# A gated network whose down weights are unpacked one step later, with first rows and first queries prepared sooner

## The reference

```python
x = x + L0_xattn(layernorm(x), ctx, ctx, gamma)         # 8 heads across the sequence axis, softmax
x = x + L0_ffn(layernorm(x), gate_up_packed, gate_up_scales, down_packed, down_scales)
x = x + L1_xattn(layernorm(x), ctx, Wq, bq, Wkv, bkv, Wp, bp)    # 16 heads, q, k, v rounded to 8 bits
x = x + L1_ffn(layernorm(x), w1, b1, w2, b2)                      # ternary weights

def L0_ffn(x, ...):                                     # inner width 1408
    w_gu, w_down = dequant_fp4(gate_up_packed), dequant_fp4(down_packed)   # 8 four-bit values a word,
    gate, up = split(x @ w_gu.T)                                           # a scale for each 128 inputs
    h = silu(gate) * up
    y = h @ w_down.T
    return y / sqrt(mean(y * y) + 1e-6)
```

## Time and profile before

| | |
|---|---|
| time, median of 3 runs | 1807.99 us (1805.15 to 1809.25) |
| time of the profiled execution | 1810.08 us |
| its span, first to last instruction | 1808.3 us |
| busy share of the span: TensorE, VectorE, ScalarE, GpSimd | 94%, 83%, 70%, 50% |
| mean granted TensorE clock | 0.992 |
| row mixing | to about 347 us |
| gated network | 351 to about 678 us |
| keys, values, queries | 678 to about 871 us |

### The profile page before, as it was taken

How to read it: one execution, slowest core, us unless ns; L and a number is a source line. 1 busy time by engine, 2 the same in 40 slices (tenths; PEclk the granted TensorE clock), 3 DMA queues, 4 the chain that set the end, 5 groups by cost and what they waited for, 6 DMA issues and landing times.

```text
span 1808.3 us, 30397 instructions
## 1 busy us (share of the span) xinstructions
PE 1705.6 (94%) x10706; PEld 744.1 (41%) x10706; DVE 1498.9 (83%) x2796; ACT 1258.2 (70%) x2111; POOL 906.5 (50%) x927
## 2 busy tenths in 40 slices
PE   4999999889999999899999999999999998999999
PEld 1332323234444444344444444444444444444444
DVE  6899999877767669688999999999999998883332
ACT  5888888455554432334799999999999996774433
POOL 6567667256444330000488888888888884000000
PEclk9999999989999999999999999999999999999999
DMA  9866651301011005557676665666666567112020
GB/s 225 214 152 134 159 137 42 111 9 24 1 24 33 32 1 168 93 105 130 115 109 109 106 109 105 115 112 112 117 112 109 105 110 239 24 24 47 24 47 24
DMA packets 420631, 170.45 MB, mean 94 GB/s; under 512 B 382080, under 2 KB 391296, under 8 KB 419328
## 3 DMA queue, kind: packets, MB, share of 16 engines
q1 hardware_dynamic: 420480, 168.51, 45.5%
HBM read 69.89 MB, written 4.19 MB: 41 GB/s over the span
## 4 chain that ended last, share of the span: by engine, by line
PE 46%; DVE 39%; ACT 7%; issue 6%; POOL 1%; DMA 1%; SPq 0%; DVEq 0%; ACTq 0%; POOLq 0%
DVE maxima L1572 22%; PE g_psY L1075 7%; PE g_psG L1062 7%; PE t_psD L2069 6%; PE t_psU L2056 5%; DVE rmax L627 5%; ACT a_prob L1694 4%; PE k_psA L1476 3%; PE psO L762 3%; PE psE L765 2%; PE a_psM L1558 2%; PE k_psA L1458 1%; DVE rinv L368 1%; PE a_psS L1606 1%; PE psS L736 1%
## 5 line engine op out<-in xcount | busy, mean ns | idle before, releaser
L1572 DVE TENSOR_REDUCE maxima<-a_psM 128x1 f32<-128x512 f32 x1024 | 623.0, 672 | 1.9 <-PE a_psM L1558 0.4
L1694 ACT ACTIVATE a_prob<-a_psS,maxima,q_scale 128x1024 uint8<-128x1024 f32 x512 | 610.9, 1209 | 16.7 <-PE a_psS L1606 14.8
L1674 POOL CAST a_wide<-a_pairs 128x2048 int16<-128x2048 uint8 x256 | 483.4, 1897 | 98.5 <-DMA a_pairs<-a_prob 85.8
L1558 PE MATMUL a_psM<-KT,QO 128*128 128x512 bf16 x1024 | 367.0, 383 | 5.8 <-DVE maxima L1572 1.6
L1606 PE MATMUL a_psS<-KT,QO 128*128 128x512 bf16 x1024 | 305.7, 380 | 3.0 <-ACT a_prob L1694 3.0
L1618 PEld LDWEIGHTS a_psO<-V,a_wide 128*128 128x128 f16 x4096 | 175.3, 96 | 140.0 <-DVE QO L1647 22.9
L905 DVE SCALAR_TENSOR_TENSOR g_sum<-g_psG,gu_scale,g_sum 128x512 f32<-128x512 f32 x176 | 124.1, 745 | 87.2 <-PE g_psG L1062 71.8
L1618 PE MATMUL a_psO<-V,a_wide 128*128 128x32 bf16 x4096 | 181.1, 177 | 16.1 <-DVE QO L1647 15.6
L884 POOL TENSOR_TENSOR g_sum<-g_sum 128x512 f32<-128x512 f32 x88 | 126.2, 1435 | 129.4 <-DVE g_sum L905 129.4
L563 ACT ACTIVATE prob<-psT 128x512 f32<-128x512 f32 x256 | 143.1, 599 | 59.9 <-PE psT L750 59.5
L1010 ACT ACTIVATE g_sum<-g_psG,gu_scale 128x512 f32<-128x512 f32 x176 | 111.5, 682 | 104.4 <-PE g_psG L1062 103.7
(11 more groups left out here) (213 smaller groups left out, 2754.1 us busy)
## 6 DMA issues: line engine op xcount, KB each, us to landing
xs<-in_x SPq DMA_DIRECT2D x64, 256.0 KB, 6.7
cs<-in_ctx SPq DMA_DIRECT2D x64, 256.0 KB, 8.9
KT<-in_w SPq DMA_DIRECT2D x2, 4096.0 KB, 19.3
raw_gu<-in_gu SPq DMA_DIRECT2D x4, 1408.0 KB, 7.2
vs<-in_ctxT SPq DMA_DIRECT2D x16, 256.0 KB, 3.0
a_pairs<-a_prob SPq DMA_TRANSPOSE x256, 3.0
out<-x_sb SPq DMA_DIRECT2D x16, 256.0 KB, 2.6
x_sb<-in_x SPq DMA_DIRECT2D x1, 3584.0 KB, 14.8
```

Source lines behind the costliest of these rows:

```text
L1558: pe.matmul(psM[n % NM][:, :], QOf[:, i * P:(i + 1) * P], KTf[:, keys:keys + 512], start=True, stop=True).then_inc(shown, 1)
L1572: v.reduce_max(tops[i // JOIN % NB][:, i % JOIN, c:c + 1], psM[n % NM][:, :], AX.X).then_inc(topped, 1)
L1674: pool.tensor_copy(wide[i % NV][:, :, :, :].rearrange("p k c q -> p k (c q)"), both).then_inc(widened, 1)
L1694: act.activation(prob[i % NP][:, k * HK:(k + 1) * HK], psS[g % NS][:, :], ACT.Exp, scale=q_scale[:, i:i + 1], bias=bias[i // JOIN % NB][:, ...
```

## The change

- In the row mixing the high halves of the first rows are copied in units 4 to 7 of the last tile, before it was units 10 to 13.
- Blocks 12 to 15 of the gate and up weights are converted on ScalarE (`value_gu`), before on VectorE; block 12 moves from tile 14 to tile 15. TensorE waits for one of these conversions ahead of the network's first half and for all four ahead of the second.
- The table of functions that has silu is loaded ahead of the last `collect`.
- GpSimd's `finish` of tile 15 moves from the end of the row mixing to behind the sums of step 1; VectorE's `after` of tiles 14 and 15 from step 2 to step 3, `aggregate` from step 3 to 4, `invert_roots` from step 4 to 5.
- `unpack_down` of a block moves from step m to step m+1, `value_down` from the end of step m to the head of step m+2, `scale_down` from the end of step m to the head of step m+2.
- `X_ROWS` moves from value unit 10 to 9, `X_TURNS` from key tile 8 to 7.

```diff
 mix_rows:
-    FIRST = (10, 11, 12, 13)
+    FIRST = (4, 5, 6, 7)
+    LAST_GU = 12
-    UNPACK.update({NT - 2: (11, 12), NT - 1: (13, 14, 15)})
+    UNPACK.update({NT - 2: (11,), NT - 1: (12, 13, 14, 15)})
+        env["gu_valued"], env["gu_left"] = gu_valued, CH * PER - LAST_GU
+        def last_rows(pool):
+            finish(pool, NT - 1)
...
 gpsimd:
-            finish(NT - 2)
-            finish(NT - 1)
+            finish(pool, NT - 2)
 scalar:
+            def value_gu(k):
+                act.wait_ge(bits_s, bits_of(k) + 2)
+                act.activation(gu_place(k), gu_words(k).bitcast(F32), ACT.Copy, scale=2.0 ** 126).then_inc(gu_valued, 1)
...
+                    if n == 13 and j in UNPACK and UNPACK[j][0] >= LAST_GU:
+                        value_gu(UNPACK[j][0])
             turns(steps)
+            nc.scalar.preload_act_table_set(SILU_SET)
             collect(NT - 1)
+            for k in UNPACK[NT - 1][1:]:
+                value_gu(k)
 vector, unpack(k, i):
-                if i == 2:
+                if i == 2 and k < LAST_GU:
 gated_ffn, gpsimd:
+                    if 2 <= m < FG + 2:
+                        scale_down(m - 2)
                     for i in SIDES:
...
-                    if t == 0:
-                        scale_down(p)
+                    if m == 1:
+                        last_rows(pool)
 vector:
-                        if m == 2:
+                        if m == 3:
                             last_tile(v, 4 + i)
...
                     if m:
                         hidden(m - 1)
+                    if 1 <= m <= FG:
+                        unpack_down(m - 1)
                     if t == 0:
-                        unpack_down(p)
-                        if p == 3:
+                        if p == 4:
                             aggregate(v, env, 0, NT)
-                        if p == 4:
+                        if p == 5:
                             invert_roots(v, env, 0, NT)
 scalar:
+                    if 2 <= m < FG + 2:
+                        value_down(m - 2)
                     if m >= 3:
                         act.wait_ge(h_ready, m - 2)
...
                         silu(m - 1)
-                    if t == 0:
-                        value_down(p)
                     if p in SPLIT and t + 1 < NTC:
                         high_part(t + 1, SPLIT.index(p))
 tensor, gate_up(t, p, i):
+                if t == 0 and p == 0:
+                    pe.wait_ge(env["gu_valued"], env["gu_left"] - 3 + 3 * i)
 keys_values_queries:
-        X_ROWS, X_TURNS = ("v", 10), ("k", 8)
+        X_ROWS, X_TURNS = ("v", 9), ("k", 7)
```

More of the change, by code:

```diff
@@ L43 @@
 LOG_SET = "natural_log_exp_and_others"
+SILU_SET = "silu_and_others"
 Programs = namedtuple("Programs", "sync gpsimd vector scalar tensor")
@@ L343, in mix_rows @@
         gu_loaded = [sem(f"m_gu_loaded{g}") for g in range(CH)]
-        first_xn, first_hi, first_lo, scales_in = (
-            sem(f"m_{n}") for n in ("first_xn", "first_hi", "first_lo", "scales_in"))
+        first_xn, first_hi, first_lo, scales_in, gu_valued = (
+            sem(f"m_{n}") for n in ("first_xn", "first_hi", "first_lo", "scales_in", "gu_valued"))
+        env["gu_valued"], env["gu_left"] = gu_valued, CH * PER - LAST_GU
         xn, halves = xs[(NT - 3) % 3], (qs[(NT - 3) % 3], ks[(NT - 3) % 3])
@@ L368, in invert, with finish, gu_words, gu_place @@
             v.reciprocal(rinv[:, at], e_sums[j % 2][:, at]).then_inc(inverted, 1)
+        def finish(pool, j):
+            if j < 2:
+                pool.wait_ge(x_loaded, 16)
+            else:
+                pool.wait_ge(x_rest, 16)
+            pool.wait_ge(inverted, HT * (j + 1))
+            pool.tensor_tensor(weighed[j % 2][:, :], weighed[j % 2][:, :], rinv[:, :],
+                               ALU.mult).then_inc(mixed_s, 1)
+            pool.wait_ge(mixed_s, j + 1)
+            pool.tensor_tensor(x_sb[:, j, :], x_sb[:, j, :], weighed[j % 2][:, :], ALU.add).then_inc(added, 1)
+        def last_rows(pool):
+            finish(pool, NT - 1)
+        def gu_words(k):
+            return raw_gu[:, k // PER % 2, k % PER * UW:(k % PER + 1) * UW]
+        def gu_place(k):
+            return env["w_gu"][:, k // PER, k % PER * UW:(k % PER + 1) * UW]
+        def bits_of(k):
+            return 3 * min(k, LAST_GU) + 2 * max(0, k - LAST_GU)
         def after(v, j):
@@ L489, in queries @@
                                        ALU.subtract).then_inc(q_ready, 1)
-            def finish(j):
-                if j < 2:
-                    pool.wait_ge(x_loaded, 16)
-                else:
-                    pool.wait_ge(x_rest, 16)
-                pool.wait_ge(inverted, HT * (j + 1))
-                pool.tensor_tensor(weighed[j % 2][:, :], weighed[j % 2][:, :], rinv[:, :],
-                                   ALU.mult).then_inc(mixed_s, 1)
-                pool.wait_ge(mixed_s, j + 1)
-                pool.tensor_tensor(x_sb[:, j, :], x_sb[:, j, :], weighed[j % 2][:, :], ALU.add).then_inc(added, 1)
             def steps(j):
                 if has(j - 2):
-                    finish(j - 2)
+                    finish(pool, j - 2)
                 if has(j + 2):
@@ L653, in unpack @@
             def unpack(k, i):
[L655 to L656 removed]
+                words = gu_words(k)
                 if i == 0:
[L658 removed]
+                    v.wait_ge(gu_loaded[k // PER], 16)
                     move_bits(v, env, words).then_inc(bits_s, 1)
                 if i == 1:
[L661 removed]
+                    v.wait_ge(bits_s, bits_of(k) + 1)
                     keep_bits(v, words).then_inc(bits_s, 1)
[L663 to L666 removed]
+                if i == 2 and k < LAST_GU:
+                    v.wait_ge(bits_s, bits_of(k) + 2)
+                    v.tensor_scalar(gu_place(k), words.bitcast(F32), 2.0 ** 126, None, ALU.mult).then_inc(bits_s, 1)
             def first_rows():
@@ L791, in tensor @@
             turns(steps)
[L793 removed]
+        return Programs(sync, gpsimd, vector, scalar, tensor), last_tile, last_rows
 def move_bits(v, env, words):
```

14 lines of the change are left out of this document (3 added, 11 removed).

## The result

The changed kernel takes 1798.42 us (median of 5 runs, 1796.48 to 1800.12) against 1807.99 for the kernel before: a ratio of 0.9948, with a 95% interval of 0.9937 to 0.996, so 9.6 us faster. The forecast was 1798.1. The two profiled executions have spans of 1808.3 and 1796.6 us, 11.7 apart, and mean granted clocks of 0.992 and 0.997.

What follows compares the result with a forecast made beforehand. TensorE is busy 94% of the span, but stands at the network's start, in its early steps' closed ring and at the first query. Queries 7.9 plus network 2.0 give 9.9 us: 1798.1 from the median, range 1793 to 1803.5.

Steps and rivals of the forecast that it cites:

- Queries: First query tile: normalising and turns moved earlier remove a 5.6 us wait and 2.3 us of slow product, 7.9 us.
- rival D: VectorE or transposes set the pace behind the first query, so no change: 1806 to 1808 us, chance 0.06.
- The ring: Network steps: TensorE half, folds, product, unpacking, conversion, copy, scaling wait in a circle; 7.4 us before, not opened.
- rival B: Network steps 0 to 10 run at TensorE's 7.0 us, conversions finding masks a step old; 1790 to 1795, chance 0.17.
- Roots and clock: Network step 5: roots there make it 11.0 us, was 8.1; TensorE stands 4.1, a clock fall may cost 2.0.
- rival E: After the stand at (6,1) the clock stays at half through whole steps, 7.0 us each; slower, chance 0.04.
- C: Network gains nothing or loses up to 4 us: third clock fall, dearer copies, slower conversions; 1800 to 1804, chance 0.21.
- a choice between two cases: Network gain: 0.6 us with both clock falls, 4.3 with neither; 2.0 taken.
- Start of the network: End of row mixing: 4.12 us stand shrinks, ScalarE's conversions hold (0,1) until 351.6, (1,1) starts 6.8 us sooner.
- Table: Function table loaded while ScalarE waits for the last sums: counted as nothing, 2.7 us more if on the path.
- The sum: First query 7.9 plus network 2.0 make 9.9 us: 1798.1 by the median, 1800.2 by the profiled execution.
- Both falls of the clock: Network: one fall before (3,1) priced 1.7 us, one behind (6,1) 2.0; with both the network gains 0.6.

Runs made afterwards that it cites:

- the first opening: Changed kernel with ScalarE's down conversion at the end of step m ahead of the high copy, GpSimd's scaling behind its sums: 1799.91 us, ratio 0.9955.
- the next: Changed kernel with the down conversion at the end of the step and GpSimd's scaling between its two sums: 1798.21 us, ratio 0.993.
- the last: Changed kernel with late down conversion, GpSimd's scaling between sums, high copies and low parts one step later, roots in step 4: 1793.14 us, ratio 0.9906.
- the last kernel: Changed kernel with late conversion, scaling between sums, copies a step later, roots in step 4, only block 14 converted before the first scaling: 1791.58 us, ratio 0.991.
- block 14 first: Changed kernel with only block 14 converted ahead of the first scaling, blocks 13 and 15 after the scaling of (0,1): 1797.31 us, ratio 0.9945.
- the network alone: Changed kernel with X_ROWS and X_TURNS put back: 1806.96 us, ratio 0.9996.
- the copies late: Changed kernel with late down conversion, GpSimd's scaling between sums, high copies and low parts one step later: 1797.77 us, ratio 0.9934.

## Why the prediction was right

**Queries.** As predicted in mechanism and size: 7.9 forecast, 8.0 alone, and 7.9 in the full change (8.8 at the first query less the network's 3.1 is 5.7 for the gap; 2.3 more for the clock, since the product's 5.93 us fell to 3.67). The first query was put at 756.5 apart from the network; it came at 753.27 + 3.14 = 756.4. VectorE's wait of 6.75 us for this query is gone and it never set the pace, so rival D falls: the 11.06 us by which the next key tile starts sooner stand unchanged at the last query product.

**The ring stays closed.** (7,1) to (8,1) and (8,1) to (9,1) take 7.71 and 7.87 us, as forecast (7.8 to 7.9), not 7.0; rival B falls for the order as written. B named a right cause, but half of it. With the conversion's mask a step old (1,1) to (2,1) falls to 4.6 us; the steps with a half copy stay at 8.2 until the copy no longer waits for its normalisation either. What B left out is what is late next: the first opening gained nothing, since GpSimd's scaling became the wait, the next kept the ring closed through the high copy, and the last stops at 7.5 to 7.7 since VectorE's operations lengthen beside GpSimd's. The 7.5 us in sum of the last kernel hold, besides the opened ring, the roots in step 4 and block 14 first (1.3).

**Roots and clock.** (5,1) to (6,1) was put at 11.0 and took 10.85; the stand at 4.1 and was 3.8. The fall of the clock behind it was put at 2.0, and the window of 9.74 lies 1.9 over the 7.88 of the kernel with the roots in step 4. That this term came out so well is in part luck: in four other kernels with the same stand (3.79 or 3.80) that window took 8.73 to 9.03, so 0.9 to 1.2 over. The clock was back at 1.00 in the next window, so rival E falls; and no third fall came, so C does too. In the prediction this fall was a choice between two cases. The runs show that it came behind each stand of 3.8 us there, and not where TensorE stood for 2.0 us in two pieces.

**Start of the network.** The forecast was 1.0 to 1.3 us too cautious at (0,1) and (1,1): of this 0.7 were there already at M, in code that is the same in both kernels, and the sums end 0.27 us later (52.43 from M instead of 52.16) where I took 0.6 for the high copies. With the copies back in units 10 to 13 and all else as after, it is 52.83, so their new place by itself costs nothing here. The conversions took 0.72 each; I had 0.73. The wait ahead of (0,1) is the predicted one. Not said in the prediction: that they could as well have stayed on VectorE, which is 1.2 to 1.9 us better.

**Table.** It costs nothing, as I took it. The Trainium skill (ScalarE: Activation LUTs, What ACT_TABLE_LOAD costs) gives 2.66 us for a switch with its drain; the trace agrees with the 1.28 of the load and shows no drain, with 0.93 us of idle time left behind the load. No run here has the load on the path, so what it costs there stays open.

**The sum.** The network's net gain was forecast at 2.0 and measured 3.1, or 2.4 from M on (2.05 alone). The 2.0 was a choice between cases, and it hid an error of the terms. Both falls of the clock that the prediction priced came, one in step 2 and one behind the roots, and for that case its own sum says 0.6. Its terms were thus 2.5 us too low in the traces: 1.3 at (1,1), of which 0.7 lay ahead of M, 1.0 in steps 1 to 5 ((1,1) to (6,1) took 43.7 us, forecast 44.7), and 0.2 behind. With 0.6 the forecast by the median would have been 1799.5. The end of the span brought another 0.6 (940.7 to 940.1) that no step foresaw, and that lies within what this stretch varies (940.0 to 940.8 over all kernels). From the profiled execution I would have said 1800.2, 1.8 too much, which is these 1.1 and 0.6. From the median it was 1798.1 against 1798.42, nearer than the terms are: the medians fell by 9.6 and the profiled spans by 11.7, and the nearness rests on this difference too. That nearness is luck; the mechanisms are not.

**Not settled.** Why the clock falls of steps 1 to 4 come in other places (0.79 in (2,1) to (3,1) after, 0.80 and 0.72 before) was not tried by itself; I counted one fall and there was one. The place is not the code's alone: with the network alone, the same network code, the windows from (0,1) to (4,1) have 0.67, 1.00, 0.77 and 0.80, where the kernel after has 1.00, 1.00, 0.79 and 1.00. And it matters less than I priced it: (5,1) comes 0.45 us later there, from M, for two low windows more, since TensorE waits for others in most of these steps. My 1.7 for a fall in them is not borne out by this pair. Which of VectorE's operations would meet which of GpSimd's was seen only once the kernel had run.

## What to carry to other kernels

An operation moved a step later opens a ring only if what it waits for stays where it was; here mask and conversion moved together, while the conversion was to move alone, and the high copy, which waits behind the same mask, with it. Before an engine is relieved, look at who waits for its *last* item in a step, and at which operations of VectorE and GpSimd will then coincide. A stand ahead of a full TensorE can have two prices, its own length and the lower clock behind it (1.5 and 1.1 to 1.9 us for the roots), so a few small operations (the roots, 3.2 us) belong where TensorE has other work in store.

## What the runs showed of the hardware

**VectorE beside GpSimd.** The same mask of 128 x 512 took 0.43 us alone and 1.37 beside GpSimd, the product 0.68 and 1.58. In the rows with the scaling between the sums, the long shift ends at 409.87 and the long mask at 411.27, each 0.3 us behind the end of the GpSimd operation during which it started (409.59 and 411.00). The product there starts at 407.89, only 0.02 us behind the scaling, and stays at 0.68; the scaling is the longer one instead (1.72, where it takes 1.16 at 399.05 in the kernel after). Two that start so close together can thus go either way. It shows most in the row mixing, whose code ahead of tile 14 is the same in all of these kernels. In most profiled executions M lies at 294.1 to 294.8 us; in that of the roots in step 4 it lies at 297.6, in that of the copies late at 297.9, some 3.5 us later. Groups of VectorE in mixing tiles 8 and 9 (mean ns of one behind the busy time), in the kernel after:

```profile
L830 DVE TENSOR_SCALAR raw_gu<-raw_gu 128x704 int32<-128x704 int32 x2 | 2.2, 1084 | 0.0
...
L825 DVE TENSOR_SCALAR raw_gu<-raw_gu,shift 128x704 int32<-128x704 int32 x2 | 1.1, 566 | 0.0
```

and in the one with the roots in step 4:

```profile
L825 DVE TENSOR_SCALAR raw_gu<-raw_gu,shift 128x704 int32<-128x704 int32 x2 | 3.0, 1505 | 0.0
L830 DVE TENSOR_SCALAR raw_gu<-raw_gu 128x704 int32<-128x704 int32 x2 | 2.9, 1474 | 0.0
```

Shift and mask take 1505 and 1474 ns there instead of 566 and 1084: the operations of VectorE and GpSimd fall together in another way, at 20.9 us for each of these two tiles instead of 19.8, by no edit. That is about as large as most of the effects studied here, and the reason for comparing from M on. It looks like a matter of the execution and not of the kernel: of the five executions with the roots in step 4 the profiled one is the longest, by 2.2 to 3.0 us. The others have no trace, so this is not shown. What starts one pattern or the other is not settled.

**The clock.** Six of the profiled executions have a stand of 3.79 to 4.10 us ahead of (6,1). In all six the granted clock of the window behind it was 0.70 to 0.83, and the window was longer than the same step at 1.00 by 0.9 to 1.9 us. With a longest stand there of 1.51 us (roots in step 4), 2.67 us (copies late) or 3.07 us (the first kernel that opens the ring) it was 1.00. At the first query stands of 5.64 and 5.65 us were followed by a product of 5.93 and 6.41 us instead of 3.67, 2.3 and 2.7 more. So the price of a fall is not one number, even in the same code.
